# A two-layer graph network on one core: one more chunk of differences per quad is made by POOL, and the last x loads are issued later

## The chip, the core and the metric

The kernel runs on one core of a Trainium2 chip. The core has a matmul engine (PE, with its weight loads shown as PEld), a vector engine (DVE), an activation engine (ACT), a general engine (POOL), and SP, which here only issues transfers. Each engine works through its own list of instructions in order; a semaphore wait at the head of a list holds everything behind it on that engine. The metric is the time of the whole program on the device in microseconds (us). The median of three runs before the change is 1106.09 us.

## What is computed

64 graphs of 128 nodes with 128 channels go through a layer norm, a first graph layer, a second layer norm and a second graph layer. Nearly all the time is in the first layer, whose core is this:

```python
D = jnp.abs(x[:, :, None, :] - x[:, None, :, :])       # 64 x 128 x 128 x 128
h = jnp.einsum('bijc,oc->bijo', D, W1) + b1             # 64 outputs
m = jnp.mean(h, axis=(0, 1, 2)); v = jnp.mean((h - m) ** 2, axis=(0, 1, 2))
h = _leaky((h - m) / jnp.sqrt(v + EPS) * g1 + be1)
s = jnp.einsum('bijo,uo->biju', h, W2)[..., 0] + b2[0]
A = jax.nn.softmax(jnp.where(A_init > 0, s, NEG), axis=-1)
y = jnp.einsum('bij,bjc->bic', A, x)
y = y @ Wg.T + bg                                       # then batch norm, leaky
out = jnp.concatenate([x, y], axis=2) @ Wt.T + bt
```

The mean and variance of h run over all pairs of nodes of all graphs. So there is a first pass that makes every product once and gathers the statistics, and a second pass that scales the products and makes the scores.

## The kernel before

**Tiling of the first pass.** The distance |x_i - x_j| is symmetric, so only 64 shifts j - i are made. A chunk is 8 shifts of a couple of graphs, a tile of 128 channels by 2048 numbers. A couple has 8 chunks (`PER`), a quad of graphs 16 (`QCH`), and the first pass has 256 chunks (`CHUNKS`) in 16 quads. In this text "chunk k" of a quad is its k-th, from 0 to 15, and m is a chunk's place in its couple, from 0 to 7.

**A chunk's way.** First its differences are made into one of five slots (`SLOTS`), by DVE or by POOL. `subtract` (L291) holds the instructions: the large one is L301, 128 x 2048; at m = 7 it is three, a small memset (L298), a small difference (L299) and L301 with 1792 columns. For m in `MAXED` (0, 3, 6) DVE makes a maximum instead, and PE corrects for it with extra bf16 products (L821, L825). For all others ACT takes the absolute value (L617) and PE multiplies (L811). DVE reads one operand from PSUM (`node_bank`) and one from `h_ext` in SBUF; POOL reads both from `h_ext`. A slot is free for chunk n when PE has finished chunk n - 5.

**After PE.** ACT copies the products of most chunks out of PSUM (`take`, two chunks behind: L629, or L632 with L636 and a sum for m = 0 and 5), SP stores them to DRAM, and DVE takes statistics (`count`, L1144). PE may start chunk n only when the PSUM tile of chunk n - 3 has been taken.

**Who makes differences.** `POOLED` = (1, 4, 7) counts in a couple, so POOL makes chunks 1, 4, 7, 9, 12 and 15 of a quad, DVE the other ten (`BY_DVE`). The lists `before(BY_DVE, n)` and `before(POOLED, n)` turn a chunk's number into the count that a semaphore must reach.

**Other work once per quad,** placed by chunk number: POOL turns adjacency into a mask (L499, after chunks 2, 5, 10 and 13), and in the list before chunk 14 it splits off a low part (`low`, L504). ACT normalises the next quad's graphs at chunk 2 (L587, four instructions). PE transposes them (L783), copies reach `h_ext`, and at chunk 6 PE makes eight small products (L801): these stand in a quad only once and serve as its clock mark below. At three places DVE makes layer norm statistics of a group of graphs (L1082, then L1089 to L1095) and POOL takes a power of them (`deviation`, L483): before chunk 15 of quads 0, 3 and 8. DVE uses the result at L1100. At the start of quad 2 (chunk 0) DVE splits a bias into bf16 parts once (`split_bias`, L1157 to L1163).

**The tail.** The last three quads' softmax and mixing run behind the second pass, in an order that `LATE_AT` writes out by step. SP stores the last quad's distances skewed to DRAM and loads them back (L439, L444), POOL adds two halves (L540), PE sums (L961), DVE takes scores (L1270). ACT meanwhile issues 16 loads of x, 256 KB each (L702), at the steps of `LOAD_X`, and DVE adds each x to a product of PE (`fold_x`, L1295) at the steps `FOLD_AT` = 262, 264, 266, 266, 272, 274, 276, 276, 276 and later ones.

## Time and profile before

| | us |
|---|---|
| median of three runs | 1106.09 |
| lowest and highest run | 1104.12, 1106.87 |
| the profiled execution, whole | 1103.98 |
| its span in the profile | 1102.2 |
| busy: PE, DVE, ACT, POOL | 1038.2, 1029.5, 997.1, 602.6 |
| first pass, from about 15 to about 645 us of the span | about 630 |
| second pass, to about 978 us | about 333 |
| tail and second layer | about 124 |

The span runs from the first to the last instruction of the profile; the whole execution has 1.8 us around it. A view's busy time doesn't say what an engine waits for; that is read from the timeline (start, duration, what ended the idle time before it) and from the marks that return once per quad.

### The profile page before, as it was taken

The page shows a single profiled execution, that of the slowest core. Times are in us where ns is not written, and L with a number is a line of the kernel's source. Part 1 is how long each engine was busy: PE and PEld are TensorE (multiplying, and loading weights), DVE is VectorE, ACT ScalarE, POOL GpSimd, SP SyncE. Part 2 cuts the span into 40 slices and gives each one's busy share as a digit, 9 for nine tenths or more (in the row PEclk, how much of TensorE's full clock was granted, in tenths as well). Part 3 has the DMA queues.
Part 4 walks back from the last instruction along what each step waited for, and adds up shares of the span by engine and source line. Part 5 has one row for each costly group of instructions (what it writes and reads, how often), then busy time and mean ns, then how long its engine had stood idle before and what let it go on. Part 6 is the DMA issues. An engine that isn't in the chain of part 4 may idle for free.

```text
span 1102.2 us, 17255 instructions
## 1 busy us (share of the span) xinstructions
PE 1038.2 (94%) x6262; PEld 448.2 (41%) x6278; DVE 1029.5 (93%) x1334; ACT 997.1 (90%) x1252; POOL 602.6 (55%) x343
## 2 busy tenths in 40 slices
PE   5998999999999899999999989899999999988997
PEld 2333333333333333343333432233333333257886
DVE  5999999999999999999999988899999999968897
ACT  5798998999999999999999979999999999954997
POOL 5676778778777777777777720222242343321330
PEclk9999999999999999999999989999999999999999
DMA  8343544444454354454444489999999999952012
GB/s 264 142 184 140 194 163 167 180 171 186 167 187 187 135 194 168 172 200 172 182 169 185 182 305 394 329 359 328 339 330 323 341 334 318 327 163 58 21 59 77
DMA packets 99204, 234.12 MB, mean 212 GB/s; under 512 B 9136, under 2 KB 46480, under 8 KB 99120
## 3 DMA queue, kind: packets, MB, share of 16 engines
q1 hardware_dynamic: 88144, 221.35, 55.0%
q0 software_dynamic: 2240, 7.34, 1.8%
q10 hardware_dynamic: 8736, 4.33, 1.5%
q8 instruction: 51, 0.84, 0.3%
q14 instruction: 33, 0.27, 0.1%
HBM read 125.24 MB, written 107.74 MB: 211 GB/s over the span
## 4 chain that ended last, share of the span: by engine, by line
PE 45%; DVE 20%; ACT 20%; issue 10%; POOL 3%; DMA 2%; DVEq 0%; ACTq 0%; POOLq 0%
PE psum L811 20%; ACT store L698 13%; PE psum L821 11%; PE psum L825 8%; DVE store L301 7%; DVE plain_st L1144 3%; POOL store L301 2%; ACT store L617 2%; PE psum L783 1%; PE psum L801 1%; DMA score_skew<-early 1%; PE psum L928 1%; DVE bst L1328 1%; DVE early L1274 1%; DVE rows L1273 1%
## 5 line engine op out<-in xcount | busy, mean ns | idle before, releaser
L301 POOL TENSOR_TENSOR store<-h_ext 128x2048 f32<-128x2048 f32 (+1 forms) x96 | 386.3, 4026 | 96.5 <-PE psum L811 95.5
L811 PE MATMUL psum<-store,w1tt_sb 128*64 128x512 f32 x1792 | 424.4, 600 | 11.6 <-ACT store L617 10.8
L301 DVE TENSOR_TENSOR store<-psum,h_ext 128x2048 f32<-128x2048 f32 x160 | 363.6, 2272 | 0.8 <-ACT h_ext L595 0.7
L617 ACT ACTIVATE store<-store 128x2048 f32<-128x2048 f32 x160 | 305.9, 1930 | 18.4 <-DVE store L301 11.8
L698 ACT ACTIVATE store<-store,st 128x1024 f32<-128x1024 f32 x192 | 227.1, 1240 | 0.0
L811 PEld LDWEIGHTS psum<-store,w1tt_sb 128*64 128x64 f32 x1792 | 122.9, 137 | 252.6 <-issue 228.4
L821 PE MATMUL psum<-store,w_twice 128*64 128x512 f32 x768 | 200.7, 599 | 5.1 <-DVE store L301 2.9
L1144 DVE BATCH_NORM_STATS2 plain_st<-store 128x6 f32<-128x512 f32 x256 | 160.3, 676 | 0.0
L825 PE MATMUL psum<-early 128*64 128x512 bf16 x1152 | 158.1, 380 | 0.0
L301 DVE TENSOR_TENSOR store<-h_ext 128x2048 f32<-128x2048 f32 x64 | 147.1, 2299 | 7.0 <-PE psum L811 6.9
L629 ACT COPY store<-psum 128x1024 f32<-128x1024 f32 x128 | 128.6, 1026 | 16.8 <-PE psum L811 11.6
L928 PE MATMUL psum<-store,w_rows 128*32 128x512 f32 x1024 | 136.2, 608 | 4.3 <-ACT store L698 4.3
L825 PEld LDWEIGHTS psum<-early 128*64 128x64 bf16 x1152 | 69.5, 110 | 132.6 <-issue 114.3
L1144 DVE BATCH_NORM_STATS2 plain_st<-psum 128x6 f32<-128x512 f32 x128 | 82.2, 683 | 12.9 <-PE psum L811 12.9
L1177 DVE TENSOR_SCALAR store<-store 128x2048 int32<-128x2048 int32 x64 | 83.5, 1304 | 2.2
L821 PEld LDWEIGHTS psum<-store,w_twice 128*64 128x64 f32 x768 | 53.3, 137 | 63.2 <-issue 37.0
L698 ACT ACTIVATE store<-psum,st 128x1024 f32<-128x1024 f32 x64 | 76.8, 1201 | 1.1 <-PE psum L811 1.1
L540 POOL TENSOR_TENSOR early<-early 128x256 f32<-128x256 f32 x16 | 22.8, 1423 | 100.0 <-DMA early<-score_skew 100.0
L636 ACT ACTIVATE psum<-psum,st 128x1024 f32<-128x1024 f32 x64 | 70.4, 1100 | 1.1 <-DVE st L1208 1.1
L632 ACT ACTIVATE store<-psum 128x1024 f32<-128x1024 f32 x64 | 66.0, 1031 | 1.0
L499 POOL TENSOR_SCALAR no_edge<-early 128x256 uint8<-128x256 int32 x64 | 54.6, 853 | 0.0
L527 POOL DMA_DIRECT2D score_skew<-early x14 | 11.5, 822 | 72.2 <-DVE early L1256 72.0
(162 smaller groups left out, 1050.5 us busy)
## 6 DMA issues: line engine op xcount, KB each, us to landing
kept_products<-store SPq DMA_DIRECT2D x192, 512.0 KB, 2.9
store<-kept_products SPq DMA_DIRECT2D x192, 512.0 KB, 5.7
early<-score_skew POOLq DMA_DIRECT2D x14, 384.0 KB, 6.3
early<-adj SPq DMA_DIRECT2D x16, 256.0 KB, 3.5
early<-adj_t SPq DMA_DIRECT2D x16, 256.0 KB, 3.6
store<-x ACTq DMA_DIRECT2D x16, 256.0 KB, 4.6
out<-early SPq DMA_DIRECT2D x16, 256.0 KB, 2.3
score_skew<-early POOLq DMA_DIRECT2D x14, 128.0 KB, 5.7
```

The source lines that it names most:

```text
L301: return engine.tensor_tensor(t[:, :, 0:steps, :], nodes.unsqueeze(2).broadcast_to([C, 2, steps, N]), windows(h_ext[:, 2 * c, :], STEP * m ...
L617: nc.scalar.activation(t, t, ACT.Abs).then_inc(abs_ready, 1)
L629: nc.scalar.copy(kept[k % ZRING], tile).then_inc(kept_ready, 1)
L632: nc.scalar.activation(kept[k % ZRING], tile, ACT.Identity, accum_out=sum_p[:, t:t + 1])\
L636: nc.scalar.activation(tile, tile, ACT.Square, bias=sc(0), accum_out=sum_m[:, t:t + 1])\
L698: nc.scalar.activation(dst, src, ACT.Prelu, bias=sc(14), scale=sc(12), alpha=SLOPE0)\
L811: last = nc.tensor.matmul(t[MID * g:MID * g + MID, b, :], w1tt_sb[:, 0:MID], diff[slot][:, g, b * BANK:b * BANK + BANK], start=True, stop= ...
L821: nc.tensor.matmul(t[MID * g:MID * g + MID, b, :], w1_twice[:, :], diff[n % SLOTS][:, g, b * BANK:b * BANK + BANK], start=True, stop=False)
L825: last = nc.tensor.matmul(t[MID * g:MID * g + MID, b, :], y_parts[:, c % 4, s, MID * g:MID * g + MID], pair_nodes[:, k, b * BANK:b * BANK ...
L928: last = nc.tensor.matmul(score[j % 2][32 * q:32 * q + 32, :], w2_rows[:, r, :], src[:, b * BANK:b * BANK + BANK], start=(r == 0), stop=(r ...
L1144: last = nc.vector.bn_stats(plain_st[:, p, t, :], src[:, t, :])
L1177: nc.vector.tensor_scalar(bits, bits, 0x7FFFFFFF, None, ALU.bitwise_and).then_inc(diff2_ready, 1)
```

## The change

`POOLED` is now counted in a quad: (1, 4, 7, 9, 12, 13, 15). Six of the seven are those of before; chunk 13 (m = 5) goes from DVE to POOL, in each of the 16 quads. A new function counts in quads, and every wait on `diff_ready` or `pool_diff` uses it. `BY_DVE` now has nine entries per quad. Apart from that, `LOAD_X` has the same groups of loads (3, 5, 4, 4) at steps 257, 268, 272, 278 where they were at 257, 262, 268, 272.

```diff
-POOLED = (1, 4, 7)
+POOLED = (1, 4, 7, 9, 12, 13, 15)
...
-BY_DVE = tuple(m for m in range(PER) if m not in POOLED)
+BY_DVE = tuple(m for m in range(2 * PER) if m not in POOLED)
...
+def before_in_quad(kinds, n):
+
+    return n // QCH * len(kinds) + sum(1 for m in kinds if m < n % QCH)
...
-        LOAD_X = {257: range(0, 3), 262: range(3, 8), 268: range(8, 12), 272: range(12, NQ)}
+        LOAD_X = {257: range(0, 3), 268: range(3, 8), 272: range(8, 12), 278: range(12, NQ)}
...
-                if n % PER in POOLED:
+                if n % QCH in POOLED:
                     differences(n)
...
-                if n % PER in POOLED:
-                    act.wait_ge(pool_diff, before(POOLED, n) + 1)
+                if n % QCH in POOLED:
+                    act.wait_ge(pool_diff, before_in_quad(POOLED, n) + 1)
                 else:
-                    act.wait_ge(diff_ready, before(BY_DVE, n) + 1)
+                    act.wait_ge(diff_ready, before_in_quad(BY_DVE, n) + 1)
...
-                    pe.wait_ge(diff_ready, before(BY_DVE, n) + 1)
+                    pe.wait_ge(diff_ready, before_in_quad(BY_DVE, n) + 1)
...
-                if n < CHUNKS and n % PER in BY_DVE:
+                if n < CHUNKS and n % QCH in BY_DVE:
                     differences(n)
```

The lines of the new kernel stand 6 further down (L301 is L307 there). On POOL, quad 0 from chunk 9 to chunk 15, before; the brackets name the semaphores that a row waits for:

```order
L301 TENSOR_TENSOR store<-h_ext 128x2048 [waits h_ext_ready,prod_ready]
L499 TENSOR_SCALAR no_edge<-early 128x256 [waits adj_in1]
L301 TENSOR_TENSOR store<-h_ext 128x2048 [waits h_ext_ready,prod_ready]
L499 TENSOR_SCALAR no_edge<-early 128x256 [waits adj_in1]
L504 TENSOR_TENSOR early<-y_rest,early 128x2x128 [waits y_mid]
L483 TENSOR_TENSOR ln<-ln,minus_half 128x16 [waits var_ready]
L298 MEMSET store 128x2x64 [waits h_ext_ready,prod_ready]
L299 TENSOR_TENSOR store<-h_ext 128x2x64
L301 TENSOR_TENSOR store<-h_ext 128x2x896
```

The same stretch of POOL after the change:

```order
L307 TENSOR_TENSOR store<-h_ext 128x2048 [waits h_ext_ready,prod_ready]
L505 TENSOR_SCALAR no_edge<-early 128x256 [waits adj_in1]
L307 TENSOR_TENSOR store<-h_ext 128x2048 [waits h_ext_ready,prod_ready] x2
L505 TENSOR_SCALAR no_edge<-early 128x256 [waits adj_in1]
L510 TENSOR_TENSOR early<-y_rest,early 128x2x128 [waits y_mid]
L489 TENSOR_TENSOR ln<-ln,minus_half 128x16 [waits var_ready]
L304 MEMSET store 128x2x64 [waits h_ext_ready,prod_ready]
L305 TENSOR_TENSOR store<-h_ext 128x2x64
L307 TENSOR_TENSOR store<-h_ext 128x2x896
```

Chunk 13 stands right behind chunk 12, and the mask, the low part, the power (in three quads) and chunk 15 stand behind both.

On ACT, the end of the second pass, before:

```order
L706 ACTIVATE h_nat<-psum,col 128x512
L702 DMA store<-x 128x4x128 x3
L710 ACTIVATE early<-early 128x512
L702 DMA store<-x 128x4x128 x5
L706 ACTIVATE h_nat<-psum,col 128x512
L702 DMA store<-x 128x4x128 x4
L710 ACTIVATE early<-early 128x512
L702 DMA store<-x 128x4x128 x4
L706 ACTIVATE h_nat<-psum,col 128x512
```

The same stretch of ACT after the change:

```order
L712 ACTIVATE h_nat<-psum,col 128x512
L708 DMA store<-x 128x4x128 x3
L716 ACTIVATE early<-early 128x512
L712 ACTIVATE h_nat<-psum,col 128x512
L708 DMA store<-x 128x4x128 x5
L716 ACTIVATE early<-early 128x512
L708 DMA store<-x 128x4x128 x4
L712 ACTIVATE h_nat<-psum,col 128x512
L708 DMA store<-x 128x4x128 x4
```

The last three groups of loads each stand one activation further down.

## Rows read from the trace of the kernel before

**Rows 1.** Windows, an undisturbed quad: length, then busy us (count) per engine, clock, DMA.
```profile
311.85:350.13 38.28, 38.28 (x218) 14.94 (x217) 36.67 (x47) 36.87 (x43) 29.27 (x16) 1.00 0.47 179
```

**Rows 2.** Timeline of PE (start, us, engine, line): the mark L801 of nine quads.
```profile
32.21 1.10 PE L801 MATMUL psum<-w1tt_sb,h_ext 128*128 128x64 f32 x8
74.70 1.10 PE L801 MATMUL psum<-w1tt_sb,h_ext 128*128 128x64 f32 x8
116.64 1.10 PE L801 MATMUL psum<-w1tt_sb,h_ext 128*128 128x64 f32 x8
154.92 1.10 PE L801 MATMUL psum<-w1tt_sb,h_ext 128*128 128x64 f32 x8
197.01 1.10 PE L801 MATMUL psum<-w1tt_sb,h_ext 128*128 128x64 f32 x8
...
311.85 1.10 PE L801 MATMUL psum<-w1tt_sb,h_ext 128*128 128x64 f32 x8
350.13 1.10 PE L801 MATMUL psum<-w1tt_sb,h_ext 128*128 128x64 f32 x8
392.54 1.10 PE L801 MATMUL psum<-w1tt_sb,h_ext 128*128 128x64 f32 x8
...
583.95 1.10 PE L801 MATMUL psum<-w1tt_sb,h_ext 128*128 128x64 f32 x8
```

**Rows 3.** Timeline of POOL, chunks 12 to 15 of the quad of Rows 1.
```profile
317.93 4.20 POOL L301 TENSOR_TENSOR store<-h_ext 128x2048 f32<-128x2048 f32 x1 [2.77 <-PE psum L811]
322.11 0.84 POOL L499 TENSOR_SCALAR no_edge<-early 128x256 uint8<-128x256 int32 x1
323.47 0.67 POOL L504 TENSOR_TENSOR early<-y_rest,early 128x256 bf16<-128x256 f32 x1 [0.52 <-ACT early L603]
324.36 0.20 POOL L298 MEMSET store<- 128x128 f32 x1 [0.21 <-PE psum L811]
```

**Rows 4.** Timeline of POOL, ACT and PE: two quads whose chunk 15 came late.
```profile
55.28 1.92 ACT L617 ACTIVATE store<-store 128x2048 f32<-128x2048 f32 x1 [1.26 <-POOL store L301]
65.47 1.94 PE L811 MATMUL psum<-store,w1tt_sb 128*64 128x512 f32 x8 [1.18 <-ACT store L617]
365.34 3.56 POOL L483 TENSOR_TENSOR ln<-ln,minus_half 128x20 f32<-128x20 f32 x1
368.85 0.20 POOL L298 MEMSET store<- 128x128 f32 x1
373.12 1.91 ACT L617 ACTIVATE store<-store 128x2048 f32<-128x2048 f32 x1 [2.17 <-POOL store L301]
383.31 1.94 PE L811 MATMUL psum<-store,w1tt_sb 128*64 128x512 f32 x8 [1.18 <-ACT store L617]
```

**Rows 5.** Timeline of POOL and DVE around the split of the bias.
```profile
92.69 4.28 POOL L301 TENSOR_TENSOR store<-h_ext 128x2048 f32<-128x2048 f32 x1 [1.25 <-PE psum L811]
92.94 4.18 DVE L1160 TENSOR_TENSOR bt_sb<-bt_sb,bt_high 128x128 f32<-128x128 f32 x1
97.49 0.29 DVE L1160 TENSOR_TENSOR bt_sb<-bt_sb,bt_high 128x128 f32<-128x128 f32 x1
98.45 2.29 DVE L301 TENSOR_TENSOR store<-psum,h_ext 128x2048 f32<-128x2048 f32 x1
```

**Rows 6.** Line L301 on DVE in the first pass: ns min/median/max.
```profile
L301 DVE TENSOR_TENSOR store<-psum,h_ext x160: 2261/2272/2292, 11.2 to 634.9; 128x2048 f32<-128x2048 f32 x160
```

**Rows 7.** The tail: timeline of SP, ACT's queue, POOL, DVE; last, line L702's landing times.
```profile
985.21 0.36 SPq L444 DMA_DIRECT2D early<-score_skew  x1
988.44 2.05 ACTq L702 DMA_DIRECT2D store<-x  x4
990.98 0.72 POOL L540 TENSOR_TENSOR early<-early 128x256 f32<-128x256 f32 x1 [12.71 <-DMA early<-score_skew]
993.08 0.69 DVE L1270 TENSOR_TENSOR early<-psum,early 128x512 f32<-128x512 f32 x1 [3.22 <-PE psum L961]
DMA to landing us min/median/max: 3.0/4.6/6.7
```

More of the change, by code:

```diff
@@ L790, in turn @@
                 if u > 1:
-                    pe.wait_ge(diff_ready, before(BY_DVE, QCH * (u - 1)))
+                    pe.wait_ge(diff_ready, before_in_quad(BY_DVE, QCH * (u - 1)))
                 transposes(u).then_inc(turned, 1)
```

## The prediction

> **What bounds the kernel now.** I read the windows by quad first, then PE's mark once per quad, then POOL's list in one quad, then the quads in which POOL's last chunk came late. In the quad of [rows 1], between two marks, PE is busy for the whole 38.28 us, DVE for 36.67, ACT for 36.87, POOL for 29.27. So DVE and ACT have 1.6 and 1.4 us to spare and POOL 9.0. The marks [rows 2] are 38.28 us apart in ten quads: one from 116.64 to 154.92, four from 197.01 to 350.13 (153.12 / 4) and five from 392.54 to 583.95 (191.41 / 5). The other four quads take 42.49, 41.94, 42.09 and 42.41 us. All that a relieved DVE could ever give back lies in those four: 168.93 - 4 x 38.28 = 15.8 us. The 16 differences that leave DVE are 16 x 2.27 = 36.3 us of its time [rows 6], but in the ten quads PE's own work is the floor, and there they are worth nothing.
>
> **Chunk 13 on POOL: the ordinary quad.** POOL may not start chunk 12 before PE has ended chunk 7: it starts 317.93 - 311.85 = 6.08 us after the mark [rows 2, 3]. Chunk 12 holds POOL for 322.11 - 317.93 = 4.18 us. Today the mask (0.84) and the low part (0.67) follow, and POOL still idles until chunk 15 starts at 324.36 [rows 3]. Now chunk 13 stands right behind chunk 12 for another 4.18 us; its slot is free (PE ends chunk 8 while POOL makes chunk 12), and mask and low part, about 1.5 us together, follow at once. Chunk 15 then starts at 317.93 + 8.36 + 1.5 = 327.8 instead of 324.36, that is 3.4 us later.
>
> What hangs on chunk 15 is told by the two quads in which it came late today [rows 4]. Its first instruction starts at 368.85 and ACT's absolute value at 373.12: 4.27 us. Behind that one on ACT are queued the copies and squares of chunks 13 and 14, the absolute value of chunk 1 of the next quad, the four normalisations and the absolute value of chunk 2; PE starts chunk 2 at 383.31, 10.19 us after 373.12. The other such quad gives 65.47 - 55.28 = 10.19 again. From there to the mark it is 392.54 - 383.31 = 9.23 us, and 74.70 - 65.47 = 9.23. So from the start of chunk 15 to the next mark it takes at least 4.27 + 10.19 + 9.23 = 23.7 us. Today: 324.36 + 23.7 = 348.05, and the mark comes at 350.13, so chunk 15 has 2.1 us of slack. It now comes 3.4 us later, and the quad is 6.08 + 9.86 + 23.69 = 39.63 us long: **1.35 us longer than 38.28**, each time, since PE's delay moves the next quad's chunk 7, and POOL waits for that. Bounds per quad: 1.0 (hand-overs as short as durations allow, some of ACT's list done earlier) to 1.7 (POOL at its slower 4.28 us [rows 5] for both chunks and mask or low part held up). The ten quads give 10 x 1.35 = 13.5. In the stretch behind the last mark there are no normalisations, but ACT there makes a block of sums and runs without a gap, so I count the 1.35 once more: 14.9, bounds 10 to 19.
>
> **The quads that are long today.** In three of them the power (L483) stands before chunk 15: 368.85 - 365.34 = 3.51 us [rows 4], less (about 2.9) for the smaller group in quad 0. The same sum with it: 39.63 + 3.51 = 43.14 against 42.41 (+0.73) and against 42.09 (+1.05); 39.63 + 2.9 = 42.5 against 42.49 (0). So in these quads DVE's relief is lost too: today POOL waits there for ACT's low part or for DVE's variance, and chunk 13 fills that wait and a little more. The statistics before the power now run on DVE while POOL is busy, which may cost a few tenths each (below): I take +2.4 for the three, bounds +1 to +5.
>
> The fourth is that of the bias split, where DVE sets the end: its first subtraction took 4.18 us from 92.94, the second, of the same shape, 0.29 [rows 5]. The first lay wholly under POOL's difference that began at 92.69 and lasted 4.28; the second ran when POOL made no difference. I read this as DVE waiting for POOL. Today POOL idles 1.25 us before 92.69 and has a pause after it; now it works without a break: chunk 12 starts at 74.70 + 6.08 = 80.8, chunk 13 at 85.0, chunk 15 at about 90.6 and chunk 1 at 94.9, to 99.1. DVE, rid of one difference but held by PE's chunk 10, comes only some 0.7 us earlier to the split (its statistic of that chunk waits for PE; an estimate); its first subtraction then waits to 94.9, and the second to 99.1. Chunk 0's difference, 0.67 us after the second subtraction's end (97.78 to 98.45), starts at about 100.0 instead of 98.45: +1.55. If the small copies and the scaling of the split wait for POOL as well, it is 2.8, and 6.6 if a third chunk of POOL gets in front. If nothing waited, it would be -0.7. I take +2.5, near the row's own case, bounds -0.7 to +6.6.
>
> The Trainium skill, page "SBUF — State Buffer", section "Who interferes with whom", says that a DVE instruction with two SBUF inputs contends with a POOL instruction that reads SBUF, and that the second one to issue is blocked for the whole instruction; the 4.18 us agree. By it the ten-odd small instructions of the split and of the statistics are the ones at risk, and the large differences, one of whose inputs is in PSUM, are not; without it the split's term would be -0.7 and the sum 3 us lower.
>
> **The x loads.** Today the load of the skewed half takes from 985.21 to POOL's sum at 990.98, 5.8 us, among five x loads; DVE takes the scores at 993.08 [rows 7]. With the five loads behind 988.44 the half runs almost alone, 2 to 3 us faster. But `FOLD_AT` didn't move: DVE's fold of x 3 stands at step 266, in front of the scores (271), and x 3 is now the first load issued at 988.44. The landings are 3.0 at best and 4.6 in the median [rows 7]; with 3.0 to 3.7 on quiet queues it lands at 991.4 to 992.1, the fold and a statistic behind it (L1295, L1290) take 1.3 together, and the scores start at 992.8 to 993.5. One wait takes the place of the other: 0, bounds -1.5 (load of 3.0, the store sooner too) to +1.4 (4.6). The last two groups have microseconds until their folds, and their issue on ACT lies in its waits.
>
> **Sum.** 14.9 + 2.4 + 2.5 + 0 = 19.8; the last stretch's share may be hidden in part, so I take 19.5. The span becomes 1102.2 + 19.5 = 1121.7 and the profiled execution 1103.98 + 19.5 = 1123.5. That execution is 2.1 us under the median of the runs shown, and 1106.09 + 19.5 = **1125.6 us** is forecast for the median, 1.8% slower. The terms' bounds, taken as independent, give +12 to +27.
>
> **Rivals.**
>
> *DVE's relief wins* (faster). POOL idles 9 us per quad, DVE is busy 93% of the span, and in the long quads DVE stands in the chain. If POOL's chunk 15 came at most 2.1 us later than today (that is the point from which it decides), the ordinary quads would stay at 38.28 and up to 15.8 us of the long ones could go; with POOL's power still in three of them, some 5: about 1101 us. Against it: 4.18 us of new work stand in front of chunk 15 and only 0.75 us of POOL's idle time there absorbs any of it.
>
> *The lateness is hidden.* ACT has 1.4 us of idle time per quad, most of it just before the absolute value of chunk 15, where it waits for PE's copy. If some of what is queued behind could be caught up, quads would stay within 0.2 us of 38.28 and only the split and the powers would count, in part: about 1108. Against it: 10.19 us twice, without an idle gap on ACT.
>
> *POOL's longer work holds DVE up.* Beyond the split, each statistics group and each L1100 waits a POOL difference of up to 4.2 us and chunk 0 or 15 is late by that, and the split costs its 6.6: 19.5 + 4.1 + about 5 = 1134. The rule of the skill above, and its page "Perfetto Trace Analysis", section "Optimizing Scalar/DVE Operations" (moving operations between those two might not help), would go this way. Against its spread to the large differences: 160 of them lie within 2261 and 2292 ns, beside a POOL that works most of the time [rows 6].
>
> **Chances.** Forecast 0.73, relief 0.07, hidden 0.08, hold-up 0.12. A measurement of this kernel can tell about 0.3% (3.3 us) from no change. Of "hidden", some 0.04 lies within 0.3%; part of "relief" does too (0.02). So faster 0.05, same 0.06, slower 0.89. The range from 1114 to 1133 holds the forecast with its bounds and a part of the hold-up.
>
> **What would show it.** In the changed profile the mark L801 (six lines further down) should come every 39.6 us in ten quads; between 38.2 and 38.5 I am wrong. POOL should idle in one piece only behind chunk 15 of a quad, start chunk 15 some 15.9 us after the mark, and ACT's absolute value behind it should show an idle time released by POOL in nearly every quad, PE's chunk 2 one released by ACT. POOL's busy time should rise by some 67 us, DVE's fall by 36 less what it waits for POOL. The split's second subtraction should last 3 to 4 us. In the tail DVE should wait for an x load just before the scores, and these start as late after the skewed store as today. The forecast is wrong if chunk 15 doesn't hold ACT, or if DVE's waits for POOL spread.

## The result, and the profile after

The changed kernel takes 1129.24 us in the median of four runs (1128.88 to 1129.45), the kernel before, run beside it on the same chip, 1105.45 us (1104.12 to 1106.87). The ratio is 1.0212 with a 95% interval of 1.0199 to 1.0225: 2.1% slower, some 23.5 us. The profiled execution has a span of 1127.3 us, 25.1 us longer than before.

The page of the changed kernel: the span, the busy time of each engine, the chain of work that ended last (shares of the span), and two of its costliest groups (busy time, mean ns of one | idle time of the engine before them, with what ended most of it).

```profile
span 1127.3 us, 17255 instructions
PE 1044.9 (93%) x6262; PEld 449.4 (40%) x6278; DVE 1015.9 (90%) x1318; ACT 999.5 (89%) x1252; POOL 664.6 (59%) x359
...
POOL 41%; issue 22%; ACT 18%; DVE 12%; PE 5%; DMA 1%; POOLq 0%; DVEq 0%; ACTq 0%
...
L817 PE MATMUL psum<-store,w1tt_sb 128*64 128x512 f32 x1792 | 424.8, 602 | 24.1 <-ACT store L623 23.2
L623 ACT ACTIVATE store<-store 128x2048 f32<-128x2048 f32 x160 | 306.2, 1926 | 42.7 <-POOL store L307 31.1
```

POOL, which had 3% of the chain, has 41%; PE, which had 45%, has 5%. ACT's absolute values (L623) waited 31.1 us for POOL and PE's products (L817) 23.2 us for ACT: a chain POOL, ACT, PE.

The same marks as in [rows 2], PE's L807 once per quad (start, us, engine, line), in the changed kernel:

```profile
32.90 1.10 PE L807 MATMUL psum<-w1tt_sb,h_ext 128*128 128x64 f32 x8
75.85 1.10 PE L807 MATMUL psum<-w1tt_sb,h_ext 128*128 128x64 f32 x8
124.19 1.10 PE L807 MATMUL psum<-w1tt_sb,h_ext 128*128 128x64 f32 x8
...
325.69 1.10 PE L807 MATMUL psum<-w1tt_sb,h_ext 128*128 128x64 f32 x8
365.20 1.10 PE L807 MATMUL psum<-w1tt_sb,h_ext 128*128 128x64 f32 x8
...
606.20 1.10 PE L807 MATMUL psum<-w1tt_sb,h_ext 128*128 128x64 f32 x8
```

The last mark is 22.25 us later than before (606.20 against 583.95). Of these, 0.69 lie ahead of the first mark (e1 below, the same program up to there as the kernel before, has this mark at 33.39, 1.18 later than 32.21, so I give them no meaning), 12.4 in the ten ordinary quads (39.52 in place of 38.28; the first of them from 124.19 to 163.73), 2.75 in the three quads with a power, and 6.40 in the quad of the split (48.34 in place of 41.94). The other 2.9 us lie behind the last mark, in small pieces up to the end of the tail.

POOL and ACT in one ordinary quad of the changed kernel, that of the mark at 325.69 (in brackets the idle time before and its releaser), to be set beside [rows 3]:

```profile
331.77 8.36 POOL L307 TENSOR_TENSOR store<-h_ext 128x2048 f32<-128x2048 f32 x2 [2.77 <-PE psum L817]
340.09 0.85 POOL L505 TENSOR_SCALAR no_edge<-early 128x256 uint8<-128x256 int32 x1
340.91 0.68 POOL L510 TENSOR_TENSOR early<-y_rest,early 128x256 bf16<-128x256 f32 x1
341.52 0.21 POOL L304 MEMSET store<- 128x128 f32 x1
...
345.79 1.91 ACT L623 ACTIVATE store<-store 128x2048 f32<-128x2048 f32 x1 [1.14 <-POOL store L307]
...
355.98 1.94 PE L817 MATMUL psum<-store,w1tt_sb 128*64 128x512 f32 x8 [1.19 <-ACT store L623]
```

Chunks 12 and 13 run back to back, chunk 15 starts 341.52 - 325.69 = 15.83 us after the mark where it started 12.51 after it, and ACT's absolute value of it waits 1.14 for POOL. From there to PE's chunk 2 it is 355.98 - 345.79 = 10.19 us, the number of [rows 4].

The split in the changed kernel, DVE and then POOL, to be set beside [rows 5]:

```profile
92.92 3.05 DVE L1163 TENSOR_SCALAR bt_sb<-bt_sb 128x128 f32<-128x128 f32 x1
96.01 4.13 DVE L1165 CAST bt_high<-bt_sb 128x128 bf16<-128x128 f32 x1
100.17 0.39 DVE L1166 TENSOR_TENSOR bt_sb<-bt_sb,bt_high 128x128 f32<-128x128 f32 x1
100.60 0.35 DVE L1165 CAST bt_high<-bt_sb 128x128 bf16<-128x128 f32 x1
100.99 4.16 DVE L1166 TENSOR_TENSOR bt_sb<-bt_sb,bt_high 128x128 f32<-128x128 f32 x1
...
106.01 2.29 DVE L307 TENSOR_TENSOR store<-psum,h_ext 128x2048 f32<-128x2048 f32 x1
```

```profile
92.24 7.82 POOL L307 TENSOR_TENSOR store<-h_ext 128x1792 f32<-128x1792 f32 x2
100.01 0.87 POOL L505 TENSOR_SCALAR no_edge<-early 128x256 uint8<-128x256 int32 x1
100.82 4.18 POOL L307 TENSOR_TENSOR store<-h_ext 128x2048 f32<-128x2048 f32 x1
```

Three instructions of DVE that take 0.2 to 0.3 us by themselves last 3.05, 4.13 and 4.16 us, each to the end of one difference of POOL. The two between them ran beside POOL's mask (L505) and took 0.39 and 0.35 us. DVE's chunk 0 starts at 106.01, 7.56 us later than before, and ACT and PE wait 8.7 and 8.3 us for it.

The first small instruction of the variance (L1095, on 20 columns) waited in the same way in quad 4, and POOL's power after it waited for DVE (DVE, then POOL):

```profile
175.10 3.12 DVE L1095 TENSOR_TENSOR ln<-ln_st 128x20 f32<-128x20 f32 x1
```

```profile
179.94 3.56 POOL L489 TENSOR_TENSOR ln<-ln,minus_half 128x20 f32<-128x20 f32 x1 [0.33 <-DVE ln L1101]
```

It was the same with the other late group (3.08 and 0.33 us). In the kernel before this instruction took 0.18 us, with POOL idle.

The tail of the changed kernel: SP's load of the half, POOL's sum, DVE's fold of x 3 and DVE's last scores, to be set beside [rows 7]:

```profile
1010.04 0.36 SPq L450 DMA_DIRECT2D early<-score_skew  x1
...
1013.48 0.73 POOL L546 TENSOR_TENSOR early<-early 128x256 f32<-128x256 f32 x1 [9.76 <-DMA early<-score_skew]
...
1017.09 0.69 DVE L1301 TENSOR_TENSOR store<-psum,store 128x512 f32<-128x512 f32 x1 [3.60 <-DMA store<-x]
...
1018.30 0.67 DVE L1276 TENSOR_TENSOR early<-psum,early 128x512 f32<-128x512 f32 x1
```

The half takes 3.4 us where it took 5.8 ([rows 7]; 5.7 to 7.1 in the experiments with the old loads, e2, e3, e7, e8, e10 and e11); DVE then waits 3.60 us for x 3. The scores are 25.22 us later than before, the last y(14) ahead of them on ACT (L712 at 1014.20) 25.76: at most 0.5 us was won in that stretch. The last y statistic of the tail is 25.21 us later than before.

### The profile page after: what moved, and what is told of

It reads as the page before. It is cut to its first block, busy times and chain, and to the rows that moved or that the text cites. A ratio compares the mean times of both kernels' runs of the same rounds, so it can differ in the third digit from the quotient of the medians.

```text
span 1127.3 us, 17255 instructions
## 1 busy us (share of the span) xinstructions
PE 1044.9 (93%) x6262; PEld 449.4 (40%) x6278; DVE 1015.9 (90%) x1318; ACT 999.5 (89%) x1252; POOL 664.6 (59%) x359
## 4 chain that ended last, share of the span: by engine, by line
POOL 41%; issue 22%; ACT 18%; DVE 12%; PE 5%; DMA 1%; POOLq 0%; DVEq 0%; ACTq 0%
POOL store L307 34%; ACT store L704 16%; POOL no_edge L505 4%; DVE store L307 3%; POOL store L305 1%; DVE bst L1334 1%; DVE early L1280 1%; DVE rows L1279 1%; DVE bst L1296 1%; POOL early L510 1%; PE psum L817 1%; DVE h_nat L1331 1%; DVE early L1276 1%; ACT h_nat L712 1%; DMA store<-x 1%
## 5 line engine op out<-in xcount | busy, mean ns | idle before, releaser
L307 POOL TENSOR_TENSOR store<-h_ext 128x2048 f32<-128x2048 f32 (+1 forms) x112 | 452.1, 4049 | 65.6 <-PE psum L817 64.7
L817 PE MATMUL psum<-store,w1tt_sb 128*64 128x512 f32 x1792 | 424.8, 602 | 24.1 <-ACT store L623 23.2
L623 ACT ACTIVATE store<-store 128x2048 f32<-128x2048 f32 x160 | 306.2, 1926 | 42.7 <-POOL store L307 31.1
L307 DVE TENSOR_TENSOR store<-psum,h_ext 128x2048 f32<-128x2048 f32 x144 | 327.4, 2274 | 0.8 <-ACT h_ext L601 0.7
L817 PEld LDWEIGHTS psum<-store,w1tt_sb 128*64 128x64 f32 x1792 | 123.2, 137 | 263.6 <-issue 246.3
L827 PE MATMUL psum<-store,w_twice 128*64 128x512 f32 x768 | 205.1, 611 | 11.2 <-DVE store L307 9.0
L307 DVE TENSOR_TENSOR store<-h_ext 128x2048 f32<-128x2048 f32 x64 | 147.5, 2305 | 6.7 <-PE psum L817 6.7
L546 POOL TENSOR_TENSOR early<-early 128x256 f32<-128x256 f32 x16 | 19.1, 1194 | 101.1 <-DMA early<-score_skew 101.1
L505 POOL TENSOR_SCALAR no_edge<-early 128x256 uint8<-128x256 int32 x64 | 54.8, 857 | 0.0
```

The source lines that it names most:

```text
L307: return engine.tensor_tensor(t[:, :, 0:steps, :], nodes.unsqueeze(2).broadcast_to([C, 2, steps, N]), windows(h_ext[:, 2 * c, :], STEP * m ...
L505: nc.gpsimd.tensor_scalar(no_edge[v % 2][:, b:b + 2, :], adj_sb[v % 2][:, 2 * half:2 * half + 2, :], 0.0, None, ALU.is_le).then_inc(edges_ ...
L623: nc.scalar.activation(t, t, ACT.Abs).then_inc(abs_ready, 1)
L817: last = nc.tensor.matmul(t[MID * g:MID * g + MID, b, :], w1tt_sb[:, 0:MID], diff[slot][:, g, b * BANK:b * BANK + BANK], start=True, stop= ...
L827: nc.tensor.matmul(t[MID * g:MID * g + MID, b, :], w1_twice[:, :], diff[n % SLOTS][:, g, b * BANK:b * BANK + BANK], start=True, stop=False)
```

## Experiments

Each is compared with runs of the kernel before beside it on its own chip; these differ by up to 1.3 us from set to set, so kernels of different sets are compared by their ratios, and by medians only roughly. Quads are differences of successive marks, in us, each named by the quad in which the second mark stands: ordinary (ten), quad 1 (with the first power, which stands before chunk 15 of quad 0), quad 2 (with the split), quads 4 and 9 (with the statistics and powers of the two late groups, before chunk 15 of quads 3 and 8).

| kernel | median | ratio, 95% interval | ordinary | 1 | 2 | 4 | 9 |
|---|---|---|---|---|---|---|---|
| before | 1105.45 | 1 | 38.28 | 42.49 | 41.94 | 42.09 | 42.41 |
| changed | 1129.24 | 1.0212 (1.0199 to 1.0225) | 39.52 | 42.95 | 48.34 | 43.39 | 43.40 |
| e1 loads only | 1106.07 | 0.9999 (0.9987 to 1.0010) | 38.29 | 42.49 | 41.94 | 42.08 | 42.39 |
| e2 POOL only | 1130.05 | 1.0215 (1.0190 to 1.0240) | 39.52 | 42.97 | 48.46 | 43.38 | 43.40 |
| e3 chunk 12 twice | 1132.33 | 1.0235 (1.0215 to 1.0255) | 39.64 | 42.88 | 48.63 | 43.36 | 43.55 |
| e4 mask, low part behind 15 | 1116.43 | 1.0087 (1.0068 to 1.0106) | 38.88 | 43.28 | 43.41 | 43.39 | 43.43 |
| e5 mask behind chunk 1 | 1111.44 | 1.0056 (1.0037 to 1.0074) | 38.28 | 42.49 | 48.27 | 42.61 | 42.62 |
| e6 changed, split late | 1121.99 | 1.0151 (1.0128 to 1.0175) | 39.53 | 42.98 | 39.54 | 43.40 | 43.42 |
| e7 before, split late | 1103.62 | 0.9983 (0.9972 to 0.9994) | 38.28 | 42.51 | 38.28 | 41.41 | 42.38 |
| e8 e7, powers moved | 1104.60 | 0.9991 (0.9981 to 1.0002) | 38.28 | 42.49 | 38.29 | 43.98 | 40.14 |
| e9 loads and fold | 1103.24 | 0.9976 (0.9965 to 0.9987) | 38.28 | 42.48 | 41.94 | 42.07 | 42.38 |
| e10 seven, in order | 1096.15 | 0.9916 (0.9894 to 0.9937) | 38.28 | 42.49 | 38.28 | 38.29 | 39.47 |
| e11 six, in order | 1095.46 | 0.9905 (0.9888 to 0.9923) | 38.28 | 42.48 | 38.27 | 38.28 | 40.32 |
| e12 e11 with e9's tail | 1094.34 | 0.9901 (0.9884 to 0.9917) | 38.28 | 42.48 | 38.28 | 38.28 | 40.33 |

### Which half of the change, and is it the relief or the lateness

```diff
-        LOAD_X = {257: range(0, 3), 262: range(3, 8), 268: range(8, 12), 272: range(12, NQ)}
+        LOAD_X = {257: range(0, 3), 268: range(3, 8), 272: range(8, 12), 278: range(12, NQ)}
```

> The kernel before with the new table of x loads alone; POOL and DVE as before. Theory (one wait took the place of the other): the half of the skewed scores lands 2 to 3 us earlier, DVE waits 3 to 4 us for x 3 just before the last scores, and the time is that of the kernel before within 1 us (ratio 0.999 to 1.001). Rival (the load change gave something back in the changed kernel that the pool work ate): 1 to 3 us faster. Rival (it cost part of the 23 us): 1 us or more slower.

Measured 0.9999. Its trace shows the swap: the half lands 3.4 us after its issue, and the last scores start 7.83 us after it, where they started 7.87 after it before. The second run is the other half, the changed kernel with the old line:

> The changed kernel with the old table of x loads: only chunk 13 goes to POOL. Theory: all of the loss is here, 1128 to 1130 us (ratio 1.020 to 1.022), marks as in the changed kernel (39.5 in ten quads, 43.4 in three, 48.3 in the quad of the split). Rival (the loads cost some of it): 1125 to 1127.

Measured 1.0215 with the quads of the changed kernel. So the loss is chunk 13's move. The loads by themselves are neutral within 0.13%; in the changed kernel the intervals (0.25% to each side in e2) leave room for a us or two.

The third gives POOL the lateness without giving DVE the relief:

```diff
                 c, m = divmod(n, PER)
+                if n % QCH == 12:
+                    subtract(nc.gpsimd, c, m, n % SLOTS, ALU.subtract, own(c)).then_inc(repeated, 1)
+                    pool.wait_ge(repeated, n // QCH + 1)
                 subtract(nc.gpsimd, c, m, n % SLOTS, ALU.subtract, own(c)).then_inc(pool_diff, 1)
```

> The kernel before, but POOL makes chunk 12 of each quad twice before it signals it (the second time with the same result); DVE keeps chunk 13. So POOL comes to chunk 15 as late as in the changed kernel, and DVE gets no relief. Theory (only chunk 15's lateness counts, the relief is worth nothing there): ordinary quads take 39.5 us, the three with a power 43.4 to 43.9, and the time is 1128 to 1132 us. Rival (the relief gives part back, POOL's lateness costs more than 1.24 a quad): the ordinary quads take over 40 us and the time is 1135 or more. Rival (it isn't the lateness but what chunk 13 does on POOL's list to DVE, ACT and PE): the quads stay near 38.3 and the time under 1115.

POOL in an ordinary quad of it (the mark before stands at 326.65):

```profile
332.73 8.47 POOL L301 TENSOR_TENSOR store<-h_ext 128x2048 f32<-128x2048 f32 x2 [2.79 <-PE psum L815]
341.16 0.85 POOL L503 TENSOR_SCALAR no_edge<-early 128x256 uint8<-128x256 int32 x1
...
342.60 0.21 POOL L298 MEMSET store<- 128x128 f32 x1
```

The two instructions take 8.47 where two chunks took 8.36 (the wait between them), so chunk 15 starts 15.95 us after the mark, 3.44 later than before, and the quad takes 39.64: 1.36 over 38.28, which is 3.44 - 2.08, the slack of [rows 3, 4]. In the changed kernel it is 3.32 - 2.08 = 1.24, and 1.24 was measured. Even the quad of the split comes out at 48.63 without any relief of DVE (48.34 with it). So the 36 us that DVE was rid of bought 0.3 us in one quad at most. The ratio of e3 is 0.0023 above that of the changed kernel, and their intervals overlap.

### Is there a threshold

On POOL, in the changed kernel, the mask and the low part go behind chunk 15, so that chunk 15 comes within the 2.08 us of slack:

```diff
-... PLACE_AT, LOW_AT = 2, 3, 5, 6, 8, 11, 11, 12, 14
+... PLACE_AT, LOW_AT = 2, 3, 5, 6, 8, 11, 11, 12, 16
...
-                if n % PER in (2, 5):
+                if n % QCH in (2, 5, 10, 15):
                     edges(n // PER, n % PER // 5)
```

> The changed kernel, but on POOL the mask and the low part, which stand before chunk 15, stand behind it (chunks 12, 13, 15, then low part and mask). Chunk 15 then comes 1.9 us later than in the kernel before instead of 3.3, inside the 2.1 us of slack that I worked out for it. Theory (a threshold at 2.1 us): the ordinary quads go back to 38.3 to 38.5 us and PE is their floor again; three quads with a power 41 to 42; the split stays at 47 to 48: 1111 to 1117 us in all. Rival (any work ahead of chunk 15 costs its own length, no threshold): quads of 39.5 - 1.5 = 38.0, which cannot be told from the floor, but with the kernel before at 38.28 as floor the same 38.3. Rival (chunk 13's mere place on POOL costs 1.2 a quad, whatever the order): 39.5 and 1127 to 1130 us.

Neither 38.3 to 38.5 nor 39.5: the ordinary quads take 38.88. POOL, ACT and PE in one of them (mark at 317.74):

```profile
332.12 0.20 POOL L304 MEMSET store<- 128x128 f32 x1
...
336.32 0.85 POOL L505 TENSOR_SCALAR no_edge<-early 128x256 uint8<-128x256 int32 x1
337.14 0.67 POOL L510 TENSOR_TENSOR early<-y_rest,early 128x256 bf16<-128x256 f32 x1
337.77 4.21 POOL L307 TENSOR_TENSOR store<-h_ext 128x2048 f32<-128x2048 f32 x1
...
342.01 1.91 ACT L623 ACTIVATE store<-store 128x2048 f32<-128x2048 f32 x1 [0.51 <-POOL store L307]
...
347.41 1.94 PE L817 MATMUL psum<-store,w1tt_sb 128*64 128x512 f32 x8 [0.60 <-ACT store L623]
```

Chunk 15 starts 14.38 us after the mark, 1.87 later than before and inside the 2.08. (POOL's chunk 15 is the memset L304 and what follows it.) But POOL now works without a break from chunk 12 to chunk 1, and it is chunk 1 of the next quad (337.77) for which ACT waits 0.51 and, behind its four normalisations, PE 0.60. My theory had one due time; POOL's list has one for each chunk. Chunk 1 starts 20.03 us after the mark, 17.99 before the change ([rows 1] has the mark, 329.84 is its start on POOL), and is 0.60 too late: its slack is 1.44 us. The next run, the changed kernel again, leaves the low part behind chunk 15 and moves the mask, 0.85 us, behind chunk 1:

```diff
-                if n % PER in (2, 5):
+                if n % QCH in (2, 5, 10):
                     edges(n // PER, n % PER // 5)
+                if n % QCH == 1 and n > QCH or n == CHUNKS - 1:
+                    edges((n - 2) // PER if n < CHUNKS - 1 else n // PER, 1)
```

> The changed kernel, on POOL chunks 12, 13, 15, then the low part, chunk 1 of the next quad and only then the mask. In the run with mask and low part both behind chunk 15 the ordinary quads took 38.88 us: ACT waited 0.51 us for chunk 1, which the mask (0.85) had pushed back, and PE 0.60 for chunk 2. Theory (each of POOL's chunks has its own due time; 15 and 1 have just about 2 us): 0.85 us earlier, chunk 1 is in time and the ordinary quads take 38.28 to 38.4; with the powers and the split as before about 1108 to 1111 us. Rival (POOL's chunk 13 itself costs 0.6 a quad, through DVE or ACT): 38.88 again and 1115 to 1117.

In its ordinary quads (mark at 319.77) chunk 15 starts at the same 14.38 us and chunk 1 19.22 us after the mark instead of 20.03:

```profile
334.15 0.20 POOL L304 MEMSET store<- 128x128 f32 x1
...
338.99 4.19 POOL L307 TENSOR_TENSOR store<-h_ext 128x2048 f32<-128x2048 f32 x1
```

The ten quads take 38.28 again. Seven chunks on POOL cost an ordinary quad nothing if they are in this order; 1.87 us of lateness are free and 3.32 cost 1.24. Against e4 the ordinary quads gave 6.0 us and the three with a power 2.4, but the split took back 4.9, since the order of e4 had spared it a part of its waits (43.41), and this one doesn't (48.27). That leaves 3.5 us, which the ratios show too (1.0087 and 1.0056, 3.4 us); the medians, from two sets of runs, are 5.0 apart. In e4 DVE's chunk 0 behind the split starts at 100.63 (one subtraction held for 4.18 us), here at 105.07: a subtraction held for 4.18 and then a cast of 128 elements on one partition held for 4.15 us under the next difference (DVE, then POOL):

```profile
95.14 4.18 DVE L1168 TENSOR_TENSOR bt_sb<-bt_sb,bt_high 128x128 f32<-128x128 f32 x1
...
100.90 4.15 DVE L1171 CAST bt_rows<-bt_sb 1x128 bf16<-1x128 f32 x1
```

```profile
100.81 4.16 POOL L307 TENSOR_TENSOR store<-h_ext 128x2048 f32<-128x2048 f32 x1
```

### The split

```diff
-                if n == 2 * QCH:
-                    split_bias()
...
             for n in range(-LEAD_DIFF, CHUNKS + TAIL):
+                if n == 100:
+                    split_bias()
```

> The changed kernel with the bias split moved from DVE's step 32 of the first pass to its step 100 of the second, where POOL is mostly idle. Theory (three small instructions of the split each waited for a whole chunk of POOL, which cost the quad 6.4 us more than before and 8.8 more than an ordinary one): the quad that took 48.34 takes 39.5, the time is 8 to 9.5 us under the changed kernel's, 1119.5 to 1121.5. Rival (the statistics of that stretch or the first POOL chunk are the cause): the quad stays above 43 and the time above 1124. Rival (the split costs the same in the second pass): the quad falls and the time stays near 1129.

The quad falls from 48.34 to 39.54, an ordinary quad of that kernel, but the time by 7.25 us (6.7 by the ratios), not 8.8. Between DVE's last small instruction ahead of the second pass (L1246 of the changed kernel) and the end of the tail (DVE's last y statistic) 1.9 us are lost again. In the second pass of this kernel DVE is busy some 24.2 of 25 us, and the split takes 2.06 us of it even without POOL, as its rows in the next run, the kernel before with the split moved in the same way, show:

> The kernel before with the split moved in the same way. Theory: its quad falls from 41.94 to 38.3 and the time by 3.7 us, 1101.5 to 1103 us: of the 6.4 us that the change cost there, all sits in the split's waits, and before it was a smaller loss of the same kind. Rival (the quad is long for the statistics on DVE): over 41 and 1105 to 1106.

```profile
773.56 0.21 DVE L1157 TENSOR_SCALAR bt_sb<-bt_sb 128x128 f32<-128x128 f32 x1
773.80 0.23 DVE L1159 CAST bt_high<-bt_sb 128x128 bf16<-128x128 f32 x1
774.07 0.29 DVE L1160 TENSOR_TENSOR bt_sb<-bt_sb,bt_high 128x128 f32<-128x128 f32 x1
```

Here are the instructions without contention: 0.21, 0.23, 0.29 us, against 3.05, 4.13, 4.16. The quad fell to 38.28 as expected, the sum only by 1.4 to 1.9 us (expected 3.7). The profiled execution started its second pass 4.06 us earlier than before and ended its tail no earlier. ACT's L706, once per quad there, tells where that went: it is 3.3 us ahead of the kernel before up to the split, 1.5 behind the split (the split's own time), 1.9 at the last but one and level at the last, which waits for the skewed half. The load of that half took 7.1 us here (983.05 to 990.16) and 5.8 before. No run shows why it took longer; with the old loads it varied from kernel to kernel.

### The powers and the statistics

This kernel is e7 with two of the three powers in front of chunk 12:

```diff
-POWER_AT = (None, None, 15, 63, 143)
-SCALE_AT = (None, None, 18, 70, 150)
+POWER_AT = (None, None, 15, 75, 155)
+SCALE_AT = (None, None, 18, 80, 160)
```

> The kernel before with the split moved and two of the three powers moved on POOL from in front of chunk 15 to in front of chunk 12 (from step 63 to 75 and from 143 to 155, their scales from 70 and 150 to 80 and 160), into the 2.8 us that POOL idles there. Theory (a power of 3.5 us in front of chunk 15 exceeds the 2.1 us of slack by what the quads show, 3.8 and 4.1 us with the statistics): these two quads fall to 38.3 to 39, the sum is 1094 to 1096 us. Rival (they are long for the statistics on DVE): they stay over 41 and the time at 1101 to 1103.

One quad fell from 42.38 to 40.14, the other rose from 41.41 to 43.98: a miss, and the row that tells why is a DVE instruction on 20 columns (DVE, then POOL):

```profile
165.31 0.33 DVE L1092 TENSOR_TENSOR ln<-ln 128x20 f32<-128x20 f32 x1
165.68 3.57 DVE L1093 SCALAR_TENSOR_TENSOR ln<-ln 128x20 f32<-128x20 f32 x1
```

```profile
164.69 0.21 POOL L298 MEMSET store<- 128x128 f32 x1
...
165.57 3.64 POOL L301 TENSOR_TENSOR store<-h_ext 128x1792 f32<-128x1792 f32 x1
```

With the power in front of chunk 15, POOL had waited for DVE's variance, so the variance was never held; with the power gone, chunk 15 starts in the middle of it and holds one small instruction for 3.57 us, and DVE's large differences behind it. So in these quads there were two causes, the power before chunk 15 and DVE's small instructions. The next two kernels put the split to step 252 (where DVE has no differences left to make), the combination of the statistics to steps 57 and 137 (where POOL idles), the statistics one per step over 20 steps, and the powers before chunk 12; the first has seven chunks on POOL in the order of e5, the second six. Both have the old loads.

```diff
-STAT_AT = (None, None, 13, 60, 140)
-POWER_AT = (None, None, 15, 63, 143)
-SCALE_AT = (None, None, 18, 70, 150)
+STAT_AT = (None, None, 13, 57, 137)
+POWER_AT = (None, None, 15, 75, 155)
+SCALE_AT = (None, None, 18, 81, 161)
...
-                    first = QUAD * GROUPS[g][1] - 2 * (STAT_AT[g] - n)
-                    for b in (first, first + 1):
+                    each = 2 if g == 2 else 1
+                    first = QUAD * GROUPS[g][1] - each * (STAT_AT[g] - n)
+                    for b in range(first, first + each):
...
+                if n == 252:
+                    split_bias()
```

> POOL makes seven chunks as in the changed kernel, with its list in the order that brought the ordinary quads back to 38.28 (12, 13, 15, low part, 1, mask), the split in DVE's step 252 of the second pass (where DVE waits for loads), the statistics of the two late groups one per step over 20 steps instead of two over ten and their combination at step 57 and 137 (where POOL idles), the two powers at 75 and 155 in front of chunk 12, x loads as before. Theory (what was long in the two quads was DVE: 20 statistics of 0.23 us beside 36.7 us of other work, and small instructions that wait for POOL; with chunk 13 gone DVE has 3.9 us a quad): both quads fall to 38.3 to 39, the split's too, sum 1095 to 1098 us. Rival (POOL's power costs its 3.5 us wherever it stands): 41 to 42 in two quads, 1102 or so.

> The same moves of split, statistics and powers in the kernel before (POOL makes six chunks, DVE keeps chunk 13, POOL's mask and low part where they were). Theory (DVE has only 1.6 us a quad to spare here, and the 20 statistics cost it 3.5 us in each of the quads over which they are spread): these quads stay 1.5 to 2.5 us over 38.28 each, the sum is 1098 to 1101 us, 2 to 4 us behind the run with seven: the only place where DVE's relief pays. Rival (DVE's relief is worth nothing anywhere): the two are equal within 1 us.

Both take 9 to 10.5 us less than the kernel before: 0.9916 and 0.9905, intervals that overlap. The forecast that six chunks would be 2 to 4 us behind fell: quad 4 is at 38.28 in both. Only in quad 9 does DVE's relief show. With six chunks DVE is busy for 40.22 of its 40.32 us, with seven for 37.30 of 39.47, so there DVE is the bound and the relief pays 0.85 us. But with seven the quads in which a power stands before chunk 12 (5 and 10) take 38.83 and 38.85 instead of 38.28, 1.1 us in all: there the power (3.57) starts right behind the mask, chunk 12 starts 6.77 us after the mark instead of 6.08, and POOL works without a pause up to the end of chunk 4. In e11 the instruction that had lasted 3.57 us in quad 4 takes 0.18 in both late groups; this is the second:

```profile
347.32 0.18 DVE L1093 SCALAR_TENSOR_TENSOR ln<-ln 128x20 f32<-128x20 f32 x1
```

### The tail

The new table of loads, and the fold of x 3 behind the scores:

```diff
-        FOLD_AT = (262, 264, 266, 266, 272, 274, 276, 276, 276)
+        FOLD_AT = (262, 264, 266, 272, 272, 274, 276, 276, 276)
```

> The kernel before with the new table of x loads, and DVE's fold of x 3 moved behind the last scores (FOLD_AT from 266 to 272). Theory (the half now lands 2 to 3 us earlier and only the wait for x 3 gives that back): the last scores start 2 to 3 us earlier after the skewed store, the sum is 2 to 3 us under the kernel before, ratio 0.9973 to 0.9982. Rival (something behind the scores, ACT or the next outputs of x on PE, is late anyway, or PE's outputs for the step 272 now wait for that fold): within 1 us of the kernel before.

SP, POOL and DVE in its tail:

```profile
986.48 0.36 SPq L444 DMA_DIRECT2D early<-score_skew  x1
...
989.88 0.73 POOL L540 TENSOR_TENSOR early<-early 128x256 f32<-128x256 f32 x1 [9.38 <-DMA early<-score_skew]
...
992.21 0.69 DVE L1270 TENSOR_TENSOR early<-psum,early 128x512 f32<-128x512 f32 x1 [0.80 <-PE psum L961]
```

The half lands 3.4 us after its issue, and DVE takes the scores as soon as PE's sums are there. Ratio 0.9976, 2.6 us: the new loads are worth something only with the fold moved. The fold's move alone wasn't run; in the kernel before that fold was done long before DVE's wait of 3.22 us for the scores ([rows 7]), so it didn't hold them up there.

> The run with six chunks on POOL in the new order, with the new table of x loads and the fold of x 3 behind the last scores. The two gains lie in different stages (first pass, tail), so they should add: 1095.5 less 2.6, 1092 to 1094 us (ratio 0.988 to 0.9895). Rival (the split, now at step 252, and the new loads stand in each other's way in the tail): 1095 or more.

This is e11 with e9's loads and fold. 1094.34 us is the lowest median, but only 1.1 us under e11's, and on a chip where the kernel before is 1.3 us faster too: by their ratios the two can't be told apart. In the profiled executions the tail gained as in e9: from DVE's copy ahead of it (L1285, at 968.70) to its last y statistic 21.7 us where e11 took 24.6. But e12 was 1.15 us behind e11 when that stretch began (0.46 of it at the last mark already), and it lost 1.3 us in the layers behind. The window of 20 us that starts 20 us after that statistic (busy time of each engine and its instructions, granted clock, DMA share, GB/s), first e11's:

```profile
1012.18:1032.18 20.00, 19.21 (x136) 16.77 (x137) 16.52 (x77) 18.35 (x56) 7.81 (x5) 0.91 0.05 16
```

and e12's:

```profile
1010.41:1030.41 20.00, 19.20 (x124) 16.76 (x125) 15.26 (x75) 17.23 (x53) 7.81 (x5) 0.83 0.05 15
```

PE did 124 matmuls instead of 136 in the same 19.2 us, at a granted clock of 0.83 instead of 0.91 of its upper level, and from the last y statistic to the end it takes 1.3 us more. The dip doesn't come with the change of the tail: e9, with the same tail, has 0.91 in the same window, and e8, with the old one, has 0.86 and took 0.8 us more behind that statistic than the kernel before. What brings it on in an execution stays open.

## Why the prediction came out as it did

1125.6 us was forecast and 1129.24 measured, inside the range of 1114 to 1133; slower was given 0.89.

**Chunk 15's lateness.** Right, place and mechanism: chunk 15 came 15.8 us after the mark (forecast 15.9), ACT waited for POOL, PE's chunk 2 for ACT, and the stretches behind it were those of [rows 4]. The size was 1.24 instead of 1.35 a quad: from the end of the two chunks (8.36) to the start of chunk 15 mask and low part take 1.39, not 1.5; the slack of 2.08 held. Ten quads gave 12.4 (forecast 13.5); behind the last mark PE's last product was another 1.05 late (forecast 1.35). e3 shows that the lateness alone does it, e5 that it costs nothing once it is under the slack. What the working lacked is chunk 1's due time: in the changed kernel chunk 15 was late enough to hide it, but e4 ran into it.

**The three quads with a power.** 2.75 instead of 2.4, inside the bounds, by the same sum: the start of chunk 15 after the mark plus 23.7 gives 42.96, 43.41 and 43.42, and 42.95, 43.39 and 43.40 were measured. That DVE's small statistics collide with POOL there was in the forecast only as tenths, and by its cost that was right: in quads 4 and 9 one instruction waited 3.1 us, but POOL's power only 0.33 us for it (0.53 in quad 1). e8 shows that it can cost a quad 2.6 us.

**The split.** This is the term that was mis-sized: +6.40 instead of +2.5, at the upper bound of +6.6. I took the case in which only the two subtractions wait. The scaling (L1163 of the changed kernel) and the first cast (L1165) waited as well, 3.05 and 4.13 us, and that pushed the second subtraction under a third difference of POOL, which is the case that I had priced at 6.6 and not taken. The row that I went by, the subtraction of [rows 5], couldn't tell whether a cast waits, and the value nearest to it was the wrong choice in a list where each wait moves the next instruction into the next difference. The Trainium skill, page "SBUF — State Buffer", section "Who interferes with whom", names copy, cast and tensor_scalar among the DVE operations that can contend with POOL, and says that the second to issue is blocked for the whole instruction; the 3.05 and 4.13 us agree. Beside POOL's mask (100.01 to 100.88) the trace differs: the subtraction, with two inputs in SBUF, began at 100.17 and took 0.39 us, so it didn't wait for the mask's end.

**The x loads.** Right: 0, with the very swap that was described. DVE could fold x 3 2.9 us after its issue at 1014.21, a little sooner than the 3.0 to 3.7 allowed for, and the fold stood in front of the scores. e9 shows that the half-load's gain (5.8 to 3.4 us) is real and was only hidden by that fold.

**What wasn't in the sum.** Some 2.9 us between the last mark and the end of the tail: the last chunks late (1.05, counted above), then 0.9 more until the second pass began, since the product chunk that is made again now waited 0.90 us for ACT's last copy, and 0.9 within the second pass: ACT's first L706 there is 25.2 us later than before, and the later ones stay at 24.8 to 25.2; why, no run shows. Sum of all: 12.4 + 2.75 + 6.4 + 1.05 + 0.9 + 0.9 + 0.7 at the head = 25.1, the difference of the two spans. The profiled execution of before lay 1.5 us under its median, so 23.6 remain for the medians.

**The rivals.** *DVE's relief wins* fell for the changed kernel by the condition that it named (chunk 15 at most 2.1 us later), and e5, where the condition holds, shows that the second half of it was wrong: with the ordinary quads back at 38.28, its long quads stay at 42.5 to 48.3 us, since they were long for POOL's power and for small instructions of DVE that wait for POOL, and relief of DVE's large differences helps neither. *The lateness is hidden* fell. *POOL's longer work holds DVE up* was right about DVE's small instructions: besides the split's, the first of the variance waited in two quads (3.12 and 3.08 us), and the scaling behind the power lasted 2.30, 3.10 and 3.10 us (0.16, 2.85 and 3.10 before). That is one reason why DVE's busy time fell by 13.6 us only. But its price held for the split alone: the variance cost the two quads 0.33 us each, and the scalings nothing, since chunk 15's start accounts for these quads to 0.02 us. The large differences kept 2.27 us (144 of them, mean 2274 ns).

## What to carry to other kernels

An engine with 9 us of idle time in a period of 38 can still have no room: what counts is the slack of each item in its list up to its due time, here 2.08 us for one chunk and 1.44 us for the next, and putting work that nobody waits for (the mask) behind the items with a due time made the room that the idle time only promised. Relieving an engine that is 93% busy gained almost nothing, because PE's work was the floor in ten quads and single waits, not load, made the others long; it paid 0.85 us in the one quad where DVE had no idle time left (quad 9 of e10 against e11). Small two-operand, cast, copy and scaling instructions of DVE belong where POOL makes no differences: moving the split, two groups of statistics and two powers gave 10 us.

## What the runs showed that I had not expected

A DVE scaling (128x128 f32 in place, 0.21 us alone) and a cast from f32 to bf16 (0.23 us alone) waited for POOL's difference to its end as the two-input subtraction did: 3.05 and 4.13 us. A cast of 128 elements on a single partition (0.22 us alone) took 4.15 us. An instruction on 20 columns of 128 partitions with two SBUF inputs (0.18 us alone) lasted 3.57 us in e8, and another of them 3.12 and 3.08 us in the changed kernel. Beside POOL's mask (a one-input instruction, int32 to uint8, 0.85 us) a cast took 0.35 and a subtraction 0.39 us, at most 0.12 longer than alone, and the subtraction was over 0.3 us ahead of the mask's end; in e5 two copies of 128 elements took 0.42 and 0.44 us beside it (0.18 alone), so short waits do occur there. And a wait that looks like a loss can protect: POOL's power, which waited for DVE's variance, kept POOL's next difference off the small instructions that make that variance.
